# A written order for the last attention group of each batch, with places for the next batch's x tiles

## What is computed

```
x = x + attn0(layernorm(x)) @ wo0
x = x + mixing_ffn(layernorm(x))        # 4 streams, 50 Sinkhorn steps
x = x + attn1(layernorm(x)) @ wo1
x = x + expert_ffn(layernorm(x))

def attn(x):                            # 32 query heads of 32, 8 key/value heads, causal
    q, k, v = rope(x @ wq), rope(x @ wk), x @ wv
    p = softmax(mask(q @ k.T / sqrt(32)))
    return p @ v
```

## Time and profile before

| | |
|---|---|
| median of 3 runs (lowest to highest) | 2952.16 us (2950.13 to 2953.05) |
| the profiled execution: its time, its span | 2949.29 us, 2947.6 us |
| TensorE busy | 2588.3 us, 88% of the span |
| VectorE, ScalarE, GpSimd busy | 62%, 37%, 38% of the span |
| mean granted TensorE clock | 0.941 of 2.4 GHz |
| last group, ahead form (2 times), first score matmul to the first matmul of the next prologue | 68.2 us, 69.8 us |
| last group, other form (2 times), first score matmul to the last store | 38.4 us, 37.8 us |

### The profile page before, as it was taken

How to read it: one execution, slowest core, us unless ns; L and a number is a source line. 1 busy time by engine, 2 the same in 40 slices (tenths; PEclk the granted TensorE clock), 3 DMA queues, 4 the chain that set the end, 5 groups by cost and what they waited for, 6 DMA issues and landing times. The chain is left out here.

```text
span 2947.6 us, 50657 instructions
## 1 busy us (share of the span) xinstructions
PE 2588.3 (88%) x15056; PEld 1807.8 (61%) x15056; DVE 1821.9 (62%) x4485; ACT 1082.8 (37%) x2317; POOL 1123.7 (38%) x801
## 2 busy tenths in 40 slices
PE   7999997999998899553759999978999987996999
PEld 6665644765553688542647555536665644885887
DVE  5677775567774433788766766764677773215443
ACT  2345554154555211442511545542355554002000
POOL 7456553555664000000044655536456552002110
PEclk9999998999999899666979999989999998998999
DMA  4323312432320521000134322223232313434111
GB/s 163 102 84 84 95 49 68 147 92 66 102 69 30 180 71 43 0 0 7 80 128 135 86 83 85 79 73 110 77 96 78 103 42 138 141 121 150 65 64 44
DMA packets 121079, 252.95 MB, mean 86 GB/s; under 512 B 12720, under 2 KB 39728, under 8 KB 120880
## 3 DMA queue, kind: packets, MB, share of 16 engines
q1 hardware_dynamic: 120912, 251.03, 26.7%
HBM read 166.57 MB, written 84.41 MB: 85 GB/s over the span
## 5 line engine op out<-in xcount | busy, mean ns | idle before, releaser
L617 ACT ACTIVATE a_prob<-a_pst 128x512 f32<-128x512 f32 (+3 forms) x1536 | 660.9, 493 | 572.2 <-PE a_pst L898 566.4
L710 DVE CUSTOM_DVE_ANT_0 a_psh<-a_psh,a_edge 128x128 f32<-128x128 f32 (+3 forms) x1024 | 480.1, 516 | 198.0 <-PE a_psh L851 170.6
L851 PE MATMUL a_psh<-a_kst,a_qst 127*128 127x512 f32 (+3 forms) x1536 | 485.3, 364 | 26.3 <-DVE a_mx L710 14.4
L898 PE MATMUL a_pst<-a_qst,a_kst 128*128 128x512 f32 (+2 forms) x1536 | 487.2, 372 | 23.1 <-DMA a_qst<-rowmax 18.6
L517 POOL TENSOR_TENSOR a_prob<-a_prob 128x2048 f32<-128x2048 f32 (+1 forms) x96 | 405.6, 4225 | 242.5 <-PE a_ppv L914 242.5
L851 PEld LDWEIGHTS a_psh<-a_kst,a_qst 127*128 127x128 f32 x1536 | 272.4, 189 | 240.2 <-DVE a_mx L713 92.7
L713 DVE TENSOR_REDUCE a_mx<-a_psh 128x1 f32<-128x512 f32 x512 | 329.3, 685 | 127.3 <-PE a_psh L851 126.2
L898 PEld LDWEIGHTS a_pst<-a_qst,a_kst 128*128 128x128 f32 x1536 | 287.5, 194 | 163.9 <-ACT a_prob L617 103.5
L914 PE MATMUL a_ppv<-a_prob,a_vg 128*32 128x512 f32 (+3 forms) x3072 | 319.2, 502 | 0.0
L502 POOL TENSOR_SCALAR_AFFINE_SELECT a_prob<-a_prob 128x512 f32<-128x512 f32 x256 | 161.9, 639 | 188.1 <-ACT a_prob L617 187.9
L927 PE MATMUL a_pden<-a_prob,a_ones 128*32 128x512 f32 (+3 forms) x2304 | 220.1, 475 | 14.1 <-POOL a_prob L517 14.1
(11 more groups left out here) (227 smaller groups left out, 4164.1 us busy)
## 6 DMA issues: line engine op xcount, KB each, us to landing
a_qst<-q SPq DMA_DIRECT2D x192, 256.0 KB, 4.5
a_wraw<-in_wqkv SPq DMA_DIRECT2D x52, 512.0 KB, 4.3
q<-a_stg_hi SPq DMA_DIRECT2D x64, 256.0 KB, 2.1
q<-a_stg_lo SPq DMA_DIRECT2D x64, 256.0 KB, 2.4
a_kst<-kT SPq DMA_DIRECT2D x96, 128.0 KB, 2.6
oT<-a_oT SPq DMA_DIRECT2D x32, 256.0 KB, 2.4
oT<-a_vT SPq DMA_DIRECT2D x32, 256.0 KB, 2.9
h_oraw<-oT SPq DMA_DIRECT2D x16, 512.0 KB, 4.0
```

What stands on the lines that cost most here:

```text
L617: act.activation(prob[k % len(prob)][:, h, off:], pst[:, (k * GH + h) % 3, off:], ACT.Exp, scale=scale).then_inc(s["exp_done"], 1)
L710: part = dve.tensor_tensor_reduce(scores, scores, edge[:, BANK - n:], 1.0, 2 * MASKED, ALU.add, ALU.max, mx_hq[kc][:, h, qt:qt + 1])
L851: mm = pe.matmul(psh[:, at, i * n:(i + 1) * n], qst[par][0:P - 1, h, qt * P:(qt + 1) * P], kst[par][0:P - 1, kc * BANK:kc * BANK + n], sta ...
L898: pe.matmul(pst[:, (k * GH + h) % 3, off:], kst[par][:, ki * P:(ki + 1) * P], qst[par][:, h, qc * BANK + off:(qc + 1) * BANK], start=True, ...
```

## The change

The last group of each batch gets a list of its own, `ORDER_7`, with the steps for x written into it. Where there is no next batch, `last_group()` drops the steps that begin with X or P. Both forms therefore get the new places of `V`, `D`, `SUM` and `NORM`. The other seven groups of a batch read `ORDER` as before. No instruction is added or removed on any engine.

```diff
+ORDER_7 = """
+    ST:0.0 ST:0.1 ST:0.2 XL:0 ST:0.3 XL:1
+    ST:1.0 ST:1.1 ST:1.2 ST:1.3 V:0 XL:2
+    ST:2.0 ST:2.1 ST:2.2 XS:0 XS:1 XN:0 V:1 ST:2.3
+    ST:3.0 XS:2 ST:3.1 ST:3.2 ST:3.3 XT:0 XL:3 D:0 XN:1 XC:0 XN:2 V:2
+    ST:4.0 D:1 ST:4.1 ST:4.2 XS:3 XT:1 XC:1 D:2 XL:4 V:3 ST:4.3
+    ST:5.0 ST:5.1 XS:4 XL:5 D:3 XT:2 XN:3 XC:2 ST:5.2 V:4 XN:4 ST:5.3 SUM:4+5
+    ST:6.0 ST:6.1 ST:6.2 XS:5 XT:3 XL:6 XC:3 ST:6.3
+    ST:7.0 V:5 ST:7.1 XS:6 XL:7 XN:5 XT:4 XC:4 ST:7.2 ST:7.3 D:4+5 V:6 XN:6
+    ST:8.0 SUM:6+7 ST:8.1 XT:5 XS:7 XC:5 ST:8.2 V:7 XN:7 ST:8.3
+    ST:9.0 ST:9.1 ST:9.2 XT:6 XC:6 ST:9.3 D:6+7 V:8
+    ST:10.0 ST:10.1 NORM:0 ST:10.2 SUM:8+9 ST:10.3
+    ST:11.0 ST:11.1 XT:7 XC:7 ST:11.2 ST:11.3 V:9 D:8+9 V:10 D:10 V:11 D:11 P:n.0 NORM:1 P:n.1 P:n.2
+      P:n.3 P:n.4 P:n.5 P:n.6 P:n.7
+"""
...
-def iteration(full_s=True, proj=True, ahead=False):
+def iteration(proj=True):
...
-    if ahead:
...
+def last_group(ahead=False):
...
+    order = parsed(ORDER_7)
+    assert [step[1] for step in order if step[0] == "D"] == DENS
+    assert [step[1] for step in order if step[0] == "SUM"] == SUMS
+    return order if ahead else [step for step in order if step[0][0] not in "XP"]
...
-    pro, bodies, body6, body7 = prologue(), (iteration(), iteration()), iteration(proj=False), iteration(False, False)
-    ahead7 = iteration(False, False, True)
+    pro, bodies, body6, body7 = prologue(), (iteration(), iteration()), iteration(proj=False), last_group()
+    ahead7 = last_group(ahead=True)
```

More of the change, by code:

```diff
@@ L92 @@
 """
+ORDER_7 = """
[13 more added lines that the diff above has]
+"""
 def parsed(text):
     steps, k = [], 0
+    number = lambda x: "next" if x == "n" else int(x)
     for word in text.split():
@@ L104, in parsed @@
         elif what in ("ST", "P"):
-            steps.append((what, *(int(x) for x in rest.split("."))))
+            steps.append((what, *(number(x) for x in rest.split("."))))
         elif what in ("D", "SUM"):
@@ L109, in parsed @@
             steps.append((what, int(rest or 0)))
-    assert k == len(USES)
+    assert k in (0, len(USES))
     return steps
@@ L118 @@
 SUMS = [step[1] for step in STEPS if step[0] == "SUM"]
-def iteration(full_s=True, proj=True, ahead=False):
+def iteration(proj=True):
     left_out = set() if proj else {"P", "WL", "WS", "RK", "VG"}
[L127 to L135, removed]
-    if ahead:
[L139 to L156, removed]
+    return [step for step in STEPS if step[0] not in left_out and (proj or step not in (("HI", 0), ("LO", 0), ("RS", 0)))]
+def last_group(ahead=False):
[3 more added lines that the diff above has]
+    return order if ahead else [step for step in order if step[0][0] not in "XP"]
 def prologue():
```

## The result

The changed kernel took 2924.18 us (median of 4 runs, 2922.85 to 2928.64) against 2951.14 us for the kernel before (4 runs, 2948.19 to 2953.05). The ratio is 0.9915, interval 0.9900 to 0.9929, so 21 to 30 us less. The forecast was 2925.6.

A forecast was written before the change was run, and what follows sets the result against it. No engine is full, so waits between engines set the ahead groups' length. Savings of 12.3 + 12.9 + 6.6 - 2.2 = 29.6, less 1.5 per ahead group, give 26.6 and 2925.6 us; range 2914 to 2942 (8 in 10).

The forecast's parts named there:

- The ahead form: Last group with the next batch's x steps and projection in it: 12.3 and 12.9 us saved in the two layers.
- the walk: Step-by-step timing of the new list from measured durations; first-layer ahead group 55.9 us to the next projection against 68.2.
- the 1.5 for latencies: Taken off each ahead group's saving for some ten hand-overs of 0.1 to 0.2 us between engines.
- Rival 3: TensorE's clock falls in the ahead group's second half; kernel slower, about 2966 us; chance 0.07.
- The lock: VectorE and GpSimd share a port pair exclusively; a normalise starting inside a GpSimd sum costs the rest of the sum.
- Both near cases: Ahead group: XN:4 starts 0.1 us ahead of the first sum, uncaught; XN:6 0.3 inside the second, caught.
- The price in the bounds: If XN:4 is caught by the first sum too, 4.4 us more in each ahead group, 2934.4 us.
- The late copy: ScalarE copies tile 0 at 461.29, though its transposes began at 454.15; the next tile needs the same banks.
- The prologue: Next projection behind the ahead group: TensorE's 2.3 us wait for the weight split goes twice, plus 2.0 of clock; 6.6 saved.
- The other form: Last group without a next batch: second sum starts 2.3 us after the first's end, not 0.8; 1.1 lost, twice.
- ahead groups of 57 to 59 us: Profile sign that the forecast is right: ahead groups of this length, measured to the next prologue.
- hardly a wait of L689 for L596: Profile sign: VectorE's low parts hardly wait for ScalarE's copies, where they waited 13.3 us before.

The follow-up runs named there:

- old_list_norm_early: Kernel before with only NORM:0 moved, in the ahead form, from the group's end to behind ST:10.1; 2944.9 us, ratio 0.9979.
- old_list_xc_early: Kernel before with one rule changed, XC:i directly behind XT:i and not behind V:i+2; 2923.8 us, ratio 0.9904.
- the two NORM experiments: NORM:0 moved forward in the kernel before (2944.9 us, 0.9979); NORM:0 and NORM:1 put back to the list's end in the changed kernel (2929.6 us, 0.9936).
- cover_rotation: Changed kernel with XN:6 before XC:4, old order for the other form, and V:11, D:11, NORM:1 behind the next projection; 2912.1 us, ratio 0.9880.

## Why the prediction was right

**The total.** 2925.6 forecast, 2924.18 and in a second measurement 2926.5 measured. 26.6 us were to be saved; the ratio gives 25. The parts below give 20.8 + 6.8 - 2.2 = 25.4. That the forecast comes so near is in part luck: two of its parts came out by errors that cancel.

**The ahead form.** To the first rotation the walk gave 54.4 and 55.4, with the 1.5 for latencies 55.9 and 56.9. The two profiles of the changed kernel show 58.8, 56.3, 58.1, 56.2. The saving was 10.4 each as a mean over the groups of the earlier trace rows and of old_list_norm_early (67.7) and the eight with the new list (57.3); the forecast had 12.3 and 12.9 less 1.5, so 11.1.

The mechanism is the one of the walk; its size came out near for a reason that the walk didn't have. Over the eight groups A is 57.3, 0.9 above the walk with its allowance (56.4), and what the walk left out is the clock. The first layer of the changed kernel is 0.5 late at `XT:0`, another 1.5 at `XT:1` (6.9 us after `XT:0`, walked 5.4) and another 2.2 at the third sum (5.7 us after `XT:6`, walked 3.5). All the rest differs by 0.3 at most, so the ten hand-overs cost next to nothing, and the 1.5 taken off for them stood in for the clock by luck.

The granted clock was at half from 11.7 to 18.6 us after that group's start and from 39.1 to 45.9; in the second layer from 12.2 to 15.6 and from 39.5 to 42.9. The eight groups with this list are of these two kinds: four with the long stretches (A 57.9 to 58.9) and four with the short ones (56.1 to 56.4). Both kinds had `XT:6` at half speed, which the walk took at full speed. Rival 3 was thus a small part of the truth. The mean clock of the two ahead groups, which the prediction expected above 0.84, was 0.82 and 0.89.

**The lock.** Both near cases came out on the side where the walk had put them, by 0.21 and 0.19 us. That was in part luck, since in the first layer the walk had both sums some 2 us too early, which is more than its margins of 0.1 and 0.3. That they are steady is not luck of one run: in all eight groups with this list `XN:4` leads by 0.21 or 0.22 and `XN:6` comes 0.18 or 0.19 late. The price in the bounds, 4.4 for a caught `XN:4`, is not what the subtraction beside it gives (4.7 less 0.8 is 3.9); a caught `XN:6` costs VectorE 4.1 (4.93 less 0.80).

**The cause.** The late copy was named as the first cause and "the whole row of tiles hangs on that". old_list_xc_early shows it: with the copies behind their transposes, and the transposes that this lets move, A falls by as much as with the written list.

**The prologue.** 6.6 forecast; R gives (16.90 - 12.95) + (15.77 - 12.94) = 6.8, and the two NORM experiments 6.2 each. Right, though the split is now held by GpSimd's rotation, of which the forecast said nothing.

**The other form.** 1.1 each forecast, 1.1 each as a mean over 28 groups. The later second sum was foreseen (1.5). Not foreseen were a later first sum (0.5, walked 0.1), 0.3 more behind the third sum, and the clock, which fell behind the third sum in half of the old list's groups (1.5 to 1.7 us each) and in none of the new one's. These nearly cancel, so the size is in part luck. The one profile has 2.4 and 2.6, which also explains why its span fell by 20.7 only.

**What it didn't see.** It took the written list as a whole. It never asked what the copy alone would give, nor what the list gives away by keeping the projection's pieces behind `D:11`, where the old list filled the wait for the third sum with them. Of its signs, ahead groups of 57 to 59 us (60.3 and 57.7) and hardly a wait of L689 for L596 (5.2 us are left of 13.3) came out only in part; the others are there.

## What to carry to other kernels

When several engines read one order, look first for the step that frees a shared bank, and put it right behind the step that fills it: here one rule gave what a rewritten list gave. Before an order is frozen, look at each VectorE instruction that can be caught by a long GpSimd one, and give it some distance (0.9 us was enough here), or put it behind work that isn't caught; and when one is moved, check which others it frees or catches. Judge a us by many instances of a group, not by one profile.

## What the runs showed of the hardware that was not expected

- After the same wait of 1.5 us on TensorE (1.52 to 1.54), with the same list around it, the next `D` took 1.06 or 1.07 in nine of 18 groups and 1.65 to 1.94 in the other nine. So equal waits had different clocks behind them. The two cases part by the time since the group's start: with the first sum at 15.7 to 16.4 us the clock held, with it at 14.7 or at 16.5 to 17.1 it fell. Why was not found.
- A GpSimd sum that a normalise beat by 0.2 us took 5.03 and not 4.56; the weight split (L463), begun 0.65 us after VectorE's multiply in cover_rotation, 2.85 and not 2.40; a normalise begun 0.2 us after a sum, 4.93 and not 0.80. The one that comes second pays, on either engine.
